# Node tables ahead of the sort's loop, and four PSUM banks for filter rows

## The chip, the cores and the metric

One core of a Trainium2 chip. The metric is the device time of one execution in microseconds; the kernel before took 6792.93 us (median of 3 runs, 6779.95 to 6798.9). The engines are TensorE (PE), VectorE (DVE), ScalarE (ACT), GpSimd (POOL) and SyncE (SP, which here only issues DMAs). Matrix inputs are float32 nearly everywhere.

## What is computed

A graph layer over 12,500 nodes of 256 features and 212,500 edges:

```python
h  = maximum(layernorm(x), 0)                      # LN without weights
xn = layernorm(h) * ln_w + ln_b
w  = (silu(rbf @ w1 + b1) @ w2 + b2) * cutoff[:, None]      # one row of 256 per edge
Q, K, V = xn @ wq + bq, xn @ wk + bk, xn @ wv + bv          # 8 heads of 32
attn = softmax over the 8 heads of (Q[src] . K[dst]) / sqrt(32) * cutoff
combined = xn[dst] * w + gate * attn * V[dst]
out = x + h + segment_sum(combined, src) @ wo + bo
```

## The kernel before

It has three stages: `prep`, `edges`, `finish`. The change is in `prep` alone.

`prep` sorts the edges by source node into 98 buckets of 128 nodes. Edges lie as 128 partitions x 1664 columns. In front of the loop, DVE counts 46 buckets (`tally`, L339) and ACT the others by sums of signs (L641). PE adds the counts over partitions and DVE makes the buckets' starts from them (L359 to L378). Then `first_chunk` ranks the edges of the first 128 columns: for each of the 98 buckets a comparison (`compare`, L385), a running count into PSUM (`count_up`, L393), a predicated copy of the rank into `pos` (L400) and a copy of the last count (L401). POOL clears the last unit of every bucket with 16 indirect DMAs (L284), and SP stores 25 MB of zeros behind the records (L232), ahead of its first four loads of edge attributes on the same queue.

The loop has 13 bodies of 16 groups; a group is 8 columns (1024 edges). Bodies are written once per entry of `SEGMENTS`, some as a hardware loop. Engines have their own instruction streams and meet at semaphores only. For each group:
- PE turns the attributes (`turn`, L540), computes the hidden layer of group g+1 in two halves (`hidden`, L551), and the filter rows of group g in four quarters j (`filters`, L562) into `w_ps[j % 2]`, two banks.
- ACT applies SiLU (L668), copies turned attributes (L659), and places cutoff, destination and slot beside the rows (L676, L677).
- DVE adds b2 and copies each quarter to `rows` (L505). Between quarters it ranks the next chunk of columns; chunks are (0,1), (1,3), (3,7), (7,11), (11,13) in bodies, so body 0 ranks 98 buckets over 256 columns, later bodies fewer.
- POOL scatters each of the 8 columns' rows to its slot in HBM by an indirect DMA (`scatter`, L303). `rows` is a ring of four groups.

The node tables ride in the same loop. A batch is 9 tiles of 128 nodes, 11 batches, one a body. In the body of a batch, ACT loads x; DVE takes statistics (L427, L434), POOL a power -1/2 (L292), DVE refines it (`normaliser`, L443 to L451), ACT makes h (L688), DVE and POOL do the same over h, DVE adds x + h (L469), ACT stores it as `base` and makes z (L700). In the next body DVE multiplies by ln_w (L478) and adds ln_b (L484), and at nine of the sixteen groups (`TILE_SLOTS`) PE turns one tile (L576) and multiplies it with wk, wv and wq (`node_tables`, L584 to L590), and ACT copies the results (L747, L708, L709, L711); then ACT stores the tables.

PSUM has eight banks: `rT_ps`, two of `hid_ps`, two of `w_ps`, `tq_ps`, `kv_ps`, `cs_ps`.

`edges` then reads the sorted records unit by unit with gathered table rows, and `finish` multiplies by wo.

Of the kernel before, what the change touches and what calls it, by code (L numbers as in the profile page):

```python
# [6 lines left out]
BF16 = mybir.dt.bfloat16  # L7
# [39 lines left out]
NB = 9  # L47
BATCHES = -(-BUCKETS // NB)
LASTB = BUCKETS - (BATCHES - 1) * NB
TILE_SLOTS = (3, 4, 6, 7, 9, 10, 12, 13, 14)  # L50
# [49 lines left out]
def prep(nc, sem, x, src, dst, rbf, weight, w1, b1, w2, b2, ln_w, ln_b, wq, bq, wk, bk, wv, bv, wo, bo,  # L100
         gate, recs, table, queries, base, ident, ones_bf, iota1, wos, bparts, unit_bucket, lagged_bucket, BQ, BKV):

    with ExitStack() as st:
# [3 lines left out]
        def ps(name, shape, dt=F32):  # L107
# [38 lines left out]

        xg = sb("xg", [P, NB, H])
        hg = sb("hg", [P, NB, H])
        stats = sb("stats", [P, NB, 6])
# [6 lines left out]
        kvx = sb("kvx", [P, NB, TAB])  # L156
        qf = sb("qf", [P, NB, H])
        xnT = sb("xnT", [P, 2, P])


        early = kvx[:].rearrange("p t f -> p (t f)")
        zero = early[:, 0:ZROWS * REC]
        unit_no = early[0:BUCKETS, ZROWS * REC:ZROWS * REC + UNITS]
        src_i = early[:, ZROWS * REC + UNITS:ZROWS * REC + UNITS + CPAD].bitcast(I32)
        dst_i = qf[:].rearrange("p t f -> p (t f)")[:, 0:CPAD].bitcast(I32)
        wgt = hg[:].rearrange("p t f -> p (t f)")[:, 0:CPAD]
        bucket_i = pos[:].bitcast(I32)
        tallied = hid[:].rearrange("p a b c e -> p (a b c e)")
# [10 lines left out]
        cs_ps = ps("cs_ps", [P, TMAX])  # L179

        s = {n: sem("a_" + n) for n in (
            "filled", "consts", "src_loaded", "edges_loaded", "params_loaded", "x_loaded",
# [4 lines left out]
            "stats_done", "stats_waited", "aggregated", "ve_done", "pow_done", "small", "h_done", "base_done", "base_stored", "z_done",  # L187
            "lnw_done", "xn_done", "xnt_ps", "xnt_sb", "kv_done", "kv_out", "q_done", "q_out", "table_stored", "q_stored")}
# [6 lines left out]
        SEGMENTS = ((0, 1), (1, 2), (2, 3), (3, 7), (7, 9), (9, 10), (10, 11), (11, 12), (12, 13))  # L195
# [10 lines left out]
        def tiles_of(batch):  # L206
            return LASTB if batch == BATCHES - 1 else NB
# [4 lines left out]
        def _(sp):  # L212
# [29 lines left out]
            for q in range(RING):  # L242
                load(q, q, None)
            with sp.Fori(1, GROUPS // RING - 1) as i:
                for q in range(RING):
                    load(i * RING + q, q, i * RING + q - RING + 1)
# [73 lines left out]
        def _(dve):  # L320
# [102 lines left out]
            def statistics(of, i, lo, h, a, b):  # L423
# [4 lines left out]
                if b < n:  # L428
                    return
# [773 lines left out]
```

## Time and profile before

| | us |
|---|---|
| median of 3 runs | 6792.93 |
| the profiled execution's own time | 6810.68 |
| its span, first to last instruction | 6809.0 |
| first row copy of the loop (L505) | 252.4 |
| end of the loop | 3152 |
| PE busy | 5942.5 (87%) |

The span is that of one profiled execution. A busy PE isn't PE at its peak, and the ends of its matmuls are modelled. "Idle before" is the time in which the engine did nothing just before an instruction; behind the arrow stands what released it. "issue" and "remote" name nothing that the profile knows by an instruction.

### The profile page before, as it was taken

The numbers are of one execution on the slowest core, as the hardware profiler recorded it, in microseconds if no ns is written. First come the engines' busy times: TensorE is split into PE (matmuls) and PEld (weight loads), VectorE is DVE, ScalarE is ACT, GpSimd is POOL, SyncE is SP. The second block draws the span as 40 slices with busy tenths as digits, with TensorE's granted clock in tenths as the row PEclk, the third lists the DMA queues.
The fourth block names the chain that finished last, engine by engine and source line by source line (L and its number), as shares of the span: only waits on it lengthen the run. The fifth ranks groups of instructions, "written<-read, shape, count | busy, mean of one in ns | idle before, by whom it ended". The sixth has DMA issues, their size and how long they took to land. (4 is left out here: it accounts for less than half of the span.)

```text
span 6809.0 us, 113345 instructions
## 1 busy us (share of the span) xinstructions
PE 5942.5 (87%) x25871; PEld 4370.4 (64%) x25872; DVE 4775.8 (70%) x12885; ACT 3086.9 (45%) x11532; POOL 3695.1 (54%) x3578
## 2 busy tenths in 40 slices
PE   0479988888898889885999999999999999999999
PEld 0356555555555555554777777777777777777776
DVE  8887755454534343222888889898888899888883
ACT  5123333333333333222655555565555565555552
POOL 1366665556555555554555555555555555555550
PEclk8799999999999999997999999999999999999999
DMA  8333333334333333335888888888888888888895
GB/s 296 102 107 112 128 136 132 108 117 138 134 109 121 137 134 103 125 127 185 287 284 284 283 281 285 286 287 283 286 283 283 283 285 286 285 284 285 284 271 158
DMA packets 487479, 1426.90 MB, mean 210 GB/s; under 512 B 76933, under 2 KB 154041, under 8 KB 484163
## 3 DMA queue, kind: packets, MB, share of 16 engines
q0 software_dynamic: 230240, 977.13, 43.7%
q1 hardware_dynamic: 206208, 370.53, 16.4%
q10 hardware_dynamic: 50850, 77.03, 3.2%
q8 instruction: 91, 1.49, 0.1%
q14 instruction: 90, 0.73, 0.0%
HBM read 1074.17 MB, written 350.21 MB: 209 GB/s over the span
## 5 line engine op out<-in xcount | busy, mean ns | idle before, releaser
L842 POOL DMA_INDIRECT ukvx<-kvx_table,udst x1856 | 1892.4, 1020 | 1588.4 <-DVE uav L1031 914.1
L303 POOL DMA_INDIRECT records<-rows,slot_i x1660 | 1727.1, 1040 | 1257.8 <-DVE rows L505 702.5
L562 PE MATMUL w_ps<-w2s,hid 128*128 128x256 f32 x6656 | 1631.7, 400 | 202.2 <-DVE rows L505 182.4
L562 PEld LDWEIGHTS w_ps<-w2s,hid 128*128 128x128 f32 x6656 | 1291.7, 200 | 566.9 <-DVE rows L505 228.5
L505 DVE TENSOR_TENSOR rows<-w_ps,b2b 128x512 f32<-128x512 f32 x832 | 569.7, 686 | 1384.4 <-PE w_ps L562 631.1
L668 ACT ACTIVATE hid<-hid_ps,b1t 128x512 f32<-128x512 f32 x832 | 525.6, 683 | 1483.8 <-PE hid_ps L551 719.4
L876 ACT ACTIVATE uexp<-uscores,umax 128x8 f32<-128x8 f32 x1856 | 542.4, 293 | 1377.6 <-issue 973.3
L930 PE MATMUL uq_ps<-aggr,uonehotT 128*128 (+1 forms) x3712 | 990.1, 389 | 137.3 <-issue 124.3
L939 PE MATMUL ag_ps<-uphys,uonehot_cut 128*128 128x256 f32 x3712 | 954.5, 380 | 0.1
L942 PE MATMUL ag_ps<-uav,uonehot 128*128 128x256 f32 x3712 | 953.6, 379 | 0.0
L989 DVE TENSOR_TENSOR uprod<-uq_ps,ukvx 128x512 f32<-128x512 f32 x928 | 640.3, 690 | 362.3 <-DMA ukvx<-kvx_table,udst 330.6
L930 PEld LDWEIGHTS uq_ps<-aggr,uonehotT 128*128 128x128 f32 x3712 | 634.1, 191 | 248.8 <-issue 194.6
L939 PEld LDWEIGHTS ag_ps<-uphys,uonehot_cut 128*128 128x128 f32 x3712 | 706.4, 190 | 96.8 <-issue 0.5
L942 PEld LDWEIGHTS ag_ps<-uav,uonehot 128*128 128x128 f32 x3712 | 706.3, 190 | 96.4
L947 PE MATMUL ag_ps<-aggr,ident 128*128 x1856 | 601.7, 406 | 124.1 <-ACT aggr L886 116.7
L551 PE MATMUL hid_ps<-rT,w1d 64*128 64x512 f32 x1664 | 485.4, 661 | 225.4 <-ACT hid L668 186.2
L1031 DVE TENSOR_TENSOR uav<-ukvx,attn_ps 128x512 f32<-128x512 f32 x928 | 637.5, 687 | 5.9
L867 ACT ACTIVATE uonehot_cut<-uonehot,urec 128x128 f32<-128x128 f32 x1856 | 635.2, 393 | 0.0
L994 DVE TENSOR_TENSOR uphys<-urec,ukvx 128x512 f32<-128x512 f32 x928 | 634.2, 683 | 0.1
L1001 DVE TENSOR_REDUCE uscores<-uprod 128x16 f32<-128x512 f32 x928 | 628.8, 678 | 0.0
L947 PEld LDWEIGHTS ag_ps<-aggr,ident 128*128 128x128 f32 x1856 | 298.4, 188 | 343.9 <-issue 313.0
L393 DVE TENSOR_TENSOR_SCAN cs_ps<-eq,run 128x512 f32<-128x512 bf16 (+2 forms) x494 | 453.2, 917 | 47.4 <-DVE run L401 23.2
(139 smaller groups left out, 6040.9 us busy)
## 6 DMA issues: line engine op xcount, KB each, us to landing
urec<-records SPq DMA_DIRECT2D x928, 260.0 KB
rbf_in<-in_edge_attr SPq DMA_DIRECT2D x207, 256.0 KB
kvx_table<-kvx ACTq DMA_DIRECT2D x10, 3456.0 KB
ukvx<-kvx_table,udst POOLq DMA_INDIRECT x1856
records<-rows,slot_i POOLq DMA_INDIRECT x1661
records<-kvx SPq DMA_DIRECT2D x1, 25480.0 KB
fbase<-x_plus_h SPq DMA_DIRECT2D x14, 896.0 KB, 7.2
out<-fout SPq DMA_DIRECT2D x13, 896.0 KB, 4.9
```

The lines of the kernel that those rows point to most:

```text
L303: pool.indirect_dma_start(recs, bass.IndirectOffsetOnAxis(ap=slot_i[:, q, t:t + 1], axis=0), rows[:, q, t, :], None).then_inc(scattered[q] ...
L562: m = pe.matmul(w_ps[j % 2][:, h, :], hid[:, k % 2, c, h, j * P:(j + 1) * P], w2s[:, c, :], start=(h == 0 and c == 0), stop=(c == 1), skip ...
L842: pool.indirect_dma_start(kvx[:, k % KVDEPTH, j, :], None, table, bass.IndirectOffsetOnAxis(ap=dst_i[:, k, j:j + 1], axis=0)).then_inc(kvx ...
L867: m = act.activation(ohc[:, k, j, :], oh[:, k, j, :], ACT.Copy, scale=rec[:, k, j, R_CUT:R_CUT + 1])
L930: m = pe.matmul(q_ps[k % 2][:, j, :], ohT[:, k % 2, j, :], aggr[:, bass.ds(b + QLAG, 1), :].rearrange("p a f -> p (a f)"), start=(j == 0), ...
L939: pe.matmul(ag_ps[k % 2][:, 0:H], ohc[:, k, j, :], phys[:, k % MDEPTH, j, :], start=(j == 0), stop=False)
L942: pe.matmul(ag_ps[k % 2][:, 0:H], oh[:, k, j, :], av[:, k % MDEPTH, j, :], start=False, stop=False)
L947: pe.matmul(ag_ps[k % 2][:, 0:H], ident[:], aggr[:, bass.ds(b, 1), :].rearrange("p a f -> p (a f)"), start=False, stop=True).then_inc(s["a ...
L989: dve.tensor_tensor(prod[:, q].rearrange("p (j h) d -> p j (h d)", j=2), q_ps[q][:], kvx[:, k % KVDEPTH, :, 0:H], ALU.mult).then_inc(s["qk ...
L994: dve.tensor_tensor(phys[:, k % MDEPTH], rec[:, k, :, 0:H], kvx[:, k % KVDEPTH, :, 2 * H:3 * H], ALU.mult).then_inc(s["phys_done"], 1)
L1001: dve.tensor_reduce(sc[:, q].rearrange("p j h -> p (j h)"), prod[:, q], AX_X, ALU.add).then_inc(s["scored"], 1)
L1031: dve.tensor_tensor(av[:, k % MDEPTH].rearrange("p j (h d) -> p j h d", h=NH), kvx[:, k % KVDEPTH, :, H:2 * H].rearrange("p j (h d) -> p j ...
```

## The change

The node tables are made in front of the loop, interleaved by hand with the tallies (batches 0 to 5), the starts (batch 6) and the first chunk's ranks (batches 7 to 13). There are 14 batches of 7 tiles; x, h and xn have two buffers each. On DVE: statistics, a third of the batch's tallies or ranks, the normaliser, a third, statistics of h, a third, and z (a two-scalar pass, ACT's before). On POOL: both powers, x + h, the products with ln_w and the sums with ln_b (DVE's before), and, in batches 8 to 11, four of the 16 indirect DMAs of zeros each. On ACT: Relu of batch b, and then the copies for the tiles of batch b-1, a share of the tallies ahead of each. On SP: all stores of base, xn, K/V and Q and the loads of x from batch 2 on. PE turns each tile one ahead and takes results into pairs of banks. The gate is multiplied into wv and bv once. The first ranks are made in fours, with four quarters of `cs_ps`. The loop keeps turn, hidden, filters, the row copies, the later chunks' ranks and the scatters, and `w_ps` has four banks, one for each quarter; `tq_ps` and `kv_ps` are gone. `SEGMENTS` has six entries, not nine.

```diff
-NB = 9
-TILE_SLOTS = (3, 4, 6, 7, 9, 10, 12, 13, 14)
+NB = 7
+THIRDS = ((0, 3), (3, 5), (5, 7))
...
-        w_ps = [ps(f"w_ps{k}", [P, 2, H]) for k in range(2)]
-        tq_ps = ps("tq_ps", [P, 4 * P])
-        kv_ps = ps("kv_ps", [P, 4 * P])
+        w_ps = [ps(f"w_ps{k}", [P, 2, H]) for k in range(4)]
+        xt_ps = [rT_ps, hid_ps[0]]
+        kv_ps = [hid_ps[1], w_ps[0][:].rearrange("p j f -> p (j f)")]
+        q_ps = [w_ps[k][:, 0, :] for k in (1, 2)]
...
-        SEGMENTS = ((0, 1), (1, 2), (2, 3), (3, 7), (7, 9), (9, 10), (10, 11), (11, 12), (12, 13))
+        SEGMENTS = ((0, 1), (1, 3), (3, 7), (7, 11), (11, 12), (12, 13))
...
# SP, behind the zeros and the first four loads of attributes
+            for b in range(BATCHES):
+                if b >= 1:
+                    sp.wait_ge(s["xn_done"], b)
+                    sp.dma_start(table[rows_of(b - 1), 2 * H:3 * H]..., xn[:, (b - 1) % 2])...
+                sp.wait_ge(s["base_done"], b + 1)
+                sp.dma_start(base[rows_of(b), :]..., xg[:, b % 2]).then_inc(s["base_stored"], 16)
+                if b >= 1:
+                    store_tables(b - 1)
+                if b + 2 < BATCHES:
+                    sp.wait_ge(s["base_stored"], b * 16 + 16)
+                    load_x(sp, b + 2)
...
# POOL
+            for b in range(BATCHES):
+                q = b % 2
+                power(b * 2 + 1, 0)
+                pool.wait_ge(s["h_done"], b * NB + NB)
+                pool.tensor_tensor(xg[:, q], xg[:, q], hg[:, q], ALU.add).then_inc(s["base_done"], 1)
+                power(b * 2 + 2, 1)
+                pool.wait_ge(s["z_done"], b * NB + NB)
+                pool.tensor_tensor(hg[:, q], hg[:, q], lnw_b..., ALU.mult).then_inc(s["lnw_done"], 1)
+                if b >= 2:
+                    pool.wait_ge(s["xnt_ps"], (b - 1) * NB)
+                    pool.wait_ge(xn_stored[q], b // 2 * 16)
+                pool.tensor_tensor(xn[:, q], hg[:, q], lnb_b..., ALU.add).then_inc(s["xn_done"], 1)
...
# DVE
+            for b in range(BATCHES):
+                a = [VBUCKETS * min(b * 3 + k, 18) // 18 for k in range(4)]
+                r = [28 * min(max((b - 7) * 3 + k, 0), 21) // 21 * 4 for k in range(4)]
+                first_statistics(b)
+                tallies(a[0], a[1])
+                ranks_first(r[0], min(r[1], BUCKETS))
+                normaliser(b, 0)
+                tallies(a[1], a[2])
+                ranks_first(r[1], min(r[2], BUCKETS))
+                if b == 0:
+                    split_biases()
+                if b == 6:
+                    starts()
+                second_statistics(b)
+                tallies(a[2], a[3])
+                ranks_first(r[2], min(r[3], BUCKETS))
+                standardise(b)
...
# PE
+            for b in range(BATCHES):
+                pe.wait_ge(s["xn_done"], b + 1)
+                node_turn(b, 0)
+                for t in range(NB):
+                    if t + 1 < NB:
+                        node_turn(b, t + 1)
+                    node_tables(b, t)
...
-                if not (isinstance(g, int) and g == 0 and j < 2):
-                    pe.wait_ge(s["w_out"], g * 4 + j - 1)
+                if not (isinstance(g, int) and g == 0):
+                    pe.wait_ge(s["w_out"], g * 4 + j - 3)
...
-                        m = pe.matmul(w_ps[j % 2][:, h, :], ...
+                        m = pe.matmul(w_ps[j][:, h, :], ...
...
# ACT
+            for b in range(BATCHES + 1):
+                share = [NT * min(b * NB + k, 6 * NB) // (6 * NB) for k in range(NB + 1)]
+                if b < BATCHES:
+                    rectify(b)
+                if b == 0:
+                    tallies(0, share[NB])
+                    act.wait_ge(s["meta_ready"], 4)
+                    continue
+                take_turned(b - 1, 0)
+                for t in range(NB):
+                    if t + 1 < NB:
+                        take_turned(b - 1, t + 1)
+                    tallies(share[t], share[t + 1])
+                    take_tables(b - 1, t)
```

`rectify(b)` waits for `small` of batch b and makes h; `take_turned` and `take_tables` wait for PE and copy; from batch 1 on `take_tables` also waits for the stores of the batch before. PE takes `totals`, `turn_ends` and `find_units` in batch 5, between tiles. DVE and ACT wait for `tails_zeroed` ahead of the loop.

## Rows read from the trace of the kernel before

**Rows 1.** Windows by stage: engines' busy us and count, clock, DMA share, GB/s.
```profile
0.00:109.00 109.00, 1.62 (x5) 1.10 (x6) 99.94 (x113) 89.65 (x108) 16.65 (x23) 1.00 0.82 300
109.00:252.40 143.40, 15.37 (x44) 6.49 (x44) 106.00 (x412) 6.37 (x11) 16.91 (x16) 0.58 0.61 186
252.40:3152.00 2899.60, 2555.95 (x10290) 1679.62 (x10288) 1432.29 (x2968) 900.56 (x2034) 1763.06 (x1677) 0.94 0.35 121
```

**Rows 2.** Timeline at the loop's start: start, us, engine, line, idle before.
```profile
250.45 2.08 PE L551 MATMUL hid_ps<-rT,w1d 64*128 64x512 f32 x4 [120.08 <-ACT hid L668]
```

**Rows 3.** Timeline of PE, 1063 to 1084: node tables, a clean group, a turn.
```profile
1063.20 0.38 PE L584 MATMUL kv_ps<-bparts,ones_bf 3*128 3x512 bf16 x1
...
1066.70 1.13 PE L551 MATMUL hid_ps<-rT,w1d 64*128 64x512 f32 x4
...
1076.52 1.13 PE L551 MATMUL hid_ps<-rT,w1d 64*128 64x512 f32 x4
...
1082.96 0.38 PE L576 MATMUL tq_ps<-ident,kvx 128*128 128x128 f32 x2
1083.18 3.62 PE L562 MATMUL w_ps<-w2s,hid 128*128 128x256 f32 x16
```

**Rows 4.** Groups by line, 0 to 3200: busy, mean ns, idle before, releasers.
```profile
L562 PE MATMUL w_ps<-w2s,hid 128*128 128x256 f32 x6656 | 1631.7, 400 | 202.2 <-DVE rows L505 182.4 <-issue 19.2
...
L688 ACT ACTIVATE hg<-xg,nb,rs 128x256 f32<-128x256 f32 x98 | 50.4, 589 | 19.8 <-DVE nb L451 19.8
...
L584 PE MATMUL kv_ps<-bparts,ones_bf 3*128 3x512 bf16 x98 | 40.1, 409 | 36.1 <-issue 19.7 <-ACT xnT L747 16.2
...
L427 DVE BATCH_NORM_STATS2 stats<-xg 128x6 f32<-128x256 f32 x98 | 34.0, 411 | 0.0
```

**Rows 5.** Timeline, 3004 to 3015, PE and ACT.
```profile
3004.44 1.13 PE L551 MATMUL hid_ps<-rT,w1d 64*128 64x512 f32 x4
...
3014.72 1.27 ACT L668 ACTIVATE hid<-hid_ps,b1t 128x512 f32<-128x512 f32 x2 [12.33 <-remote]
```

**Rows 6.** Groups of POOL: bodies 0 to 2; 3 to 10; 11 and 12.
```profile
L303 POOL DMA_INDIRECT records<-rows,slot_i x379 | 419.1, 1106 | 354.3 <-DVE rows L505 228.0 <-issue 116.2 <-ACT slot_i L677 10.1
...
L303 POOL DMA_INDIRECT records<-rows,slot_i x1023 | 1059.0, 1035 | 729.7 <-DVE rows L505 391.1 <-issue 300.4 <-ACT slot_i L677 38.2
...
L303 POOL DMA_INDIRECT records<-rows,slot_i x249 | 243.5, 978 | 173.2 <-DVE rows L505 87.3 <-issue 72.0 <-ACT slot_i L677 13.9
```

**Rows 7.** Timeline of DVE in body 0: scans with and without a row copy.
```profile
253.02 0.74 DVE L393 TENSOR_TENSOR_SCAN cs_ps<-eq,run 128x256 f32<-128x256 bf16 x1
...
254.85 0.76 DVE L393 TENSOR_TENSOR_SCAN cs_ps<-eq,run 128x256 f32<-128x256 bf16 x1
...
274.94 0.76 DVE L393 TENSOR_TENSOR_SCAN cs_ps<-eq,run 128x256 f32<-128x256 bf16 x1
...
276.45 0.76 DVE L393 TENSOR_TENSOR_SCAN cs_ps<-eq,run 128x256 f32<-128x256 bf16 x1
...
280.14 1.26 DVE L385 TENSOR_SCALAR eq<-bucket,ids 128x256 bf16<-128x256 bf16 x6
```

**Rows 8.** Front: tallies by line; POOL's copy; window of the first ranks.
```profile
L339 DVE TENSOR_SCALAR_CACHE_REDUCE eq<-bucket,ids 128x1664 bf16<-128x1664 bf16 x46 | 85.9, 1942 | 0.0
...
12.16 3.22 POOL L278 COPY meta<-hg 128x1664 f32<-128x1664 f32 x1 [0.96 <-DMA hg<-in_edge_weight]
...
150.00:200.00 50.00, 0.00 (x0) 0.00 (x0) 37.10 (x147) 0.00 (x0) 0.00 (x0) 0.50 0.92 265
```

**Rows 9.** SP's loads of attributes; the DMA packets of 16 to 60 us.
```profile
15.66 104.89 SPq L240 DMA_DIRECT2D rbf_in<-in_edge_attr  x6
...
DMA packets 1887, 14.50 MB, mean 329 GB/s; under 512 B 513, under 2 KB 1019, under 8 KB 1051
```

**Rows 10.** Windows of bodies 11 and 12.
```profile
2731.80:2950.80 219.00, 198.15 (x802) 131.02 (x801) 46.13 (x66) 62.24 (x142) 125.71 (x129) 0.94 0.35 121
2950.80:3144.30 193.50, 162.15 (x655) 110.04 (x653) 41.31 (x60) 47.83 (x105) 116.46 (x121) 0.90 0.32 110
```

More of the change, by code:

```diff
@@ L634, in _ @@
-            load_x(0, 0)
-            act.wait_ge(s["bucket_ready"], 3)
-            def tally(b, q, n):
-                if n is not None:
-                    act.wait_ge(s["counted"], n)
-                act.activation(tallied[:, q * CPAD:(q + 1) * CPAD], bucket[:], ACT.Sign, bias=cut[:, bass.ds(b, 1)],
-                               accum_out=above[:, bass.ds(b, 1)]).then_inc(s["counted"], 1)
-            for n in range(3):
-                tally(VBUCKETS + n, n % 2, n - 1 if n >= 2 else None)
@@ L645, in _, with tallies @@
-            with act.Fori(1, (BUCKETS - VBUCKETS) // 2) as i:
-                for q in range(2):
-                    tally(i * 2 + VBUCKETS + 1 + q, 1 - q, i * 2 + q)
+            load_x(act, 0)
+            act.wait_ge(s["src_loaded"], 32)
+            load_x(act, 1)
+            act.wait_ge(s["bucket_ready"], 3)
+            def tallies(begin, end):
+                for n in range(begin, end):
+                    b = VBUCKETS + n
+                    if n >= 2:
+                        act.wait_ge(s["counted"], n - 1)
+                    act.activation(tallied[:, (n % 2) * CPAD:(n % 2 + 1) * CPAD], bucket[:], ACT.Sign, bias=cut[:, b:b + 1],
+                                   accum_out=above[:, b:b + 1]).then_inc(s["counted"], 1)
@@ new lines, in rectify, with take_turned @@
+            def rectify(b):
+                act.wait_ge(s["small"], b * 10 + 5)
+                if b >= 2:
+                    act.wait_ge(s["xn_done"], b - 1)
+                for t in range(NB):
+                    act.activation(hg[:, b % 2, t, :], xg[:, b % 2, t, :], ACT.Relu, bias=nb[:, 0, t:t + 1], scale=rs[:, 0, t:t + 1]).then_inc(s["h_done"], 1)
+            def take_turned(b, t):
+                c = b * NB + t
+                act.wait_ge(s["xnt_ps"], c + 1)
+                if c >= 2:
+                    act.wait_ge(s["q_done"], c - 1)
+                act.activation(xnT[:, c % 2].rearrange("p k e -> p (k e)"), xt_ps[c % 2][:, 0:H], ACT.Copy).then_inc(s["xnt_sb"], 1)
@@ new lines, in take_tables @@
+            def take_tables(b, t):
+                c = b * NB + t
+                act.wait_ge(s["kv_done"], c + 1)
+                r = [lo for lo, _ in THIRDS].index(t) if b >= 1 and t in [lo for lo, _ in THIRDS] else None
+                if r is not None:
+                    act.wait_ge(kv_stored[r], b * 16)
+                act.activation(kv[:, t, :], kv_ps[c % 2][:, 0:2 * H], ACT.Copy).then_inc(s["kv_out"], 1)
+                act.wait_ge(s["q_done"], c + 1)
+                if r is not None:
+                    act.wait_ge(q_stored[r], b * 16)
+                act.activation(qf[:, t, :], q_ps[c % 2], ACT.Copy).then_inc(s["q_out"], 1)
```

461 lines of the change are left out of this document (220 added, 241 removed).

## The prediction

> **What bounds it now.** I read the windows by stage first [rows 1]. The span of 6809 us has three parts: a front (0 to 252), the sort's loop (252 to 3152, 2900 us), and the edge stage with the finish. The change doesn't touch the third. In the front TensorE (PE) does 17 us of work; it turns one group and then waits 120 us for the first chunk's ranks [rows 2]. In the loop PE is the busiest engine, 2556 of 2900 us. The timeline shows its cost where nothing waits [rows 3]: from one hidden matmul to the same one of the next group 9.82 us, and a node tile adds 0.22 us (two transposes) and 3.50 us (tables). So 208 x 9.82 = 2043 and 98 x 3.72 = 365 us are needed at full clock; the other 492 us of the loop are stalls: 344 us in which PE is idle (2900 less 2556), and about 148 us in which it is stretched (granted clock 0.94 on average). Of the idle time 202 us stand before filter matmuls, mostly released by DVE's row copies, 36 us before the node tables [rows 4]. The rest is uneven: now and then the engines behind PE start late though PE's records run on. ACT's activation at 3014.72 ends 12.33 us of idleness, while the hidden matmuls that it takes began at 3004.44 and lasted 1.13 us [rows 5]. I can't name the cause.
>
> **Moved away from the loop.** PE: 98 tiles, 365 us, and the 36 us of waits before them. ACT: Relu (50.4 us of records [rows 4]), z (as much), the copies of each tile, and the loads and stores of its queue. DVE: two rounds of statistics (34 us each), three wide passes and the normalisers. POOL: 22 powers of about 1.9 us. None of these engines is above 50% of the loop but POOL, and POOL loses least [rows 1]. If nothing else moved, the loop would be 2900 - 365 = **2535 us**.
>
> **Four banks of filter rows.** A filter matmul then waits for DVE's copy of the same quarter one group earlier, not two quarters earlier. That takes up delays of DVE of a few us. It gives nothing where PE itself is late or where hid_out is late. No row shows it; from below it gives 0, from above all 202 us. I take half, 101 us, since DVE loses its node passes too. With the 36 us this is 137 us of idle time; stretch follows idleness (148 / 344 = 0.43 us for each us), so another 59. That gives 2535 - 196 = 2339. I take **2360**, because of the next limits.
>
> **What is late next in the loop.** POOL issues eight scatters a group, 0.30 us apart. Their means are 1.106 us in bodies 0 to 2, 1.035 in 3 to 10, 0.978 in 11 and 12 [rows 6]: 11.25, 10.68 and 10.22 us a group, 48 x 11.25 + 128 x 10.68 + 32 x 10.22 = 2234 us. DVE in body 0 must rank 98 buckets: 1.84 us for one with a row copy between, 1.51 without, 0.21 for each compare (1.26 for six) [rows 7]. For 6.1 buckets a group this is 4 x 1.84 + 2.1 x 1.51 + 6.1 x 0.21 = 11.8 us, 189 us for the body against 227 now. So nothing below 2234 + 9 = 2243 is possible, and 2360 (11.3 us a group) is 5% above it.
>
> **The new front.** Per batch of seven tiles:
> - PE 7 x 3.72 = 26.0 us.
> - DVE: 14 statistics of 0.35 (34.0 / 98 [rows 4]), 14 aggregates of 0.08, two normalisers of 1.0, seven z passes, and small steps: about 10.5 us. z as a two-scalar pass of 256 columns has no row on DVE: I take 0.23 us, between nothing and the 0.41 of one statistics record. With 46 tallies (1.87 us apart) in six batches this is 24.8 us; with 98 ranks in seven batches, at 1.0 us each, it is 24.5 us; from 150 to 200 us DVE's 147 instructions (four a rank) are busy for 37.1 us, 1.01 a rank, and take 1.36 with their gaps, which ranks in fours should fill [rows 8].
> - ACT: Relu 3.6 (50.4 / 98 x 7 [rows 4]), copies 7 x 1.4 = 9.6, and nine tallies of 1.67 in the first six: 28 us, later 13.
> - POOL: two powers and three passes of 1792 elements. Its one-input copy of 1664 took 3.22 us [rows 8], so a pass costs from 3.5 us (a second input free) to 6.9 (twice). I take 4.5, nearer to the row; 17 us a batch.
>
> The longest is ACT's 28, then PE's 26. Each batch also has a turn: ACT rectifies batch b+1 ahead of the copies of batch b, and PE can run only two tiles ahead. I take **29.5 us a batch**. From below it is 26; from above the latency of one batch. From x to the last pass: 3.2 + 1.9 + 1.0 + 3.6 + 3.2 + 1.9 + 1.0 + 1.6 + 9 = 26 us, with 14 us of tallies between 40.
>
> The start: bucket numbers are ready at 12 us. Batch 0 then needs 26 us of latency, 13 us of tallies and 8 us of bias splitting, so its first tile is at about 58. Batch 2 comes much later. Its x is loaded by SP after base_stored of batch 0, and that store lies on SP's queue behind the 25480 KB of zeros and the first four rbf loads. Those loads are issued from 15.66 on, and from 16 to 60 us only 32 packets of 2 to 8 KB move (1051 - 1019), of 256 KB loads that have 128 each [rows 9]. The zeros move at 0.3 MB a us, so to about 105. So the store of base 0 lands at about 120, x of batch 2 at 128, its coefficients at 138. ACT rectifies batch 2 ahead of the copies of batch 1. So batch 1's tiles begin at about **141**, not at 87. The other 13 batches end at 141 + 13 x 29.5 = 525, and the loop's first row copy comes at 532: **+280 us** against 252.4. DVE's whole work from 128 on is some 300 us, so it isn't the bound. The stores (5 MB a batch) and the tail zeros (16 indirect DMAs, then in batches 8 to 11; now they hold the DMA at a share of 0.92 from 150 to 200 [rows 8]) share the DMA; they may add 10 to 20 us there, which the range takes in.
>
> **A rule that speaks against it.** POOL's copy beside DVE's first tally took 3.22 us and the tally 1.95, as the later ones (1.94) [rows 8]; but scatters are 13% longer where DVE has most work [rows 6]. The Trainium skill, "GPSIMD Engine Reference", section 8, says that GpSimd shares its SBUF interfaces with VectorE and meets contention with two-input or two-port instructions, and (section 3.1) gives 4497 ns for an add of 2048 elements. An estimate from that page is 3.9 us a pass, and twice this under contention. The trace has no two-input pass of that size on POOL. By the page's price the sum stays, since POOL is then at 15 us of 29.5; doubled it would be 27, and the front would go by the fourth case below.
>
> **The sum.** The profiled execution took 6810.7 us (span 6809.0 and 1.7 around it). 6811 + 280 - (2900 - 2360) = 6551. The median of the runs, 6792.9, is 18 us lower, so 6533.
>
> **Rivals.**
> 1. *Forecast*, 6533. For: 252 us of PE idleness in the front are filled. Chance 0.37.
> 2. *The stalls stay.* They belong to PE's own lateness [rows 5], not to banks; the loop takes 2535: 6811 + 280 - 365 - 18 = 6708. For: body 12 has no node work and still stalls [rows 10]. Chance 0.20.
> 3. *POOL becomes the bound.* Loop 2243: 6811 + 280 - 657 - 18 = 6416. For: the clean group of 9.82 lies under POOL's 10.2. Against: no body comes near it. 0.20.
> 4. *The front runs by latency*, 40 us a batch: 141 + 520 + 6 = 667, +415 us; 6811 + 415 - 540 - 18 = 6668. For: all four engines pass each batch on, twice through POOL. Its gain is gone only above 49.6 us a batch. 0.12.
> 5. *Slower: the bare network is itself slow.* Body 12 has neither node tiles nor ranks, and took 193.5 us for 15 groups, 12.9 each, more than body 11 with eight tiles less their 30 us (189 / 16 = 11.8) [rows 10]. If a loop without other work settles at that rate, it takes 189 + 192 x 12.9 = 2666: 6811 + 280 - 234 - 18 = 6839. It decides from (2620 - 189) / 192 = 12.66 us a group on. For: a clock of 0.90 and PE busy for 162 of 193 us. Against: part of that idleness is what four banks take up, and the loop as a whole less its tiles comes to 2535 / 208 = 12.2. 0.08.
> 6. *The zeros don't delay batch 2*, and batches take 27 us: 58 + 14 x 27 + 6 = 442, +190: 6443. 0.03.
>
> **The numbers.** Faster by over 0.3% (about what a measurement of this kernel can tell from no change, 20 us): cases 1 to 4 and 6, less a little for mixtures, 0.88; within it 0.03; slower 0.09. The range goes from 6400 (case 3 with 16 us off) to 6720 (case 2 with 12 more); case 5 is left out.
>
> **What would show it.** PE's first matmul of a tile near 58, a gap from about 87 to 141 with SP's load of batch 2 in it, 29.5 us from batch to batch, and the first row copy at 532. In the loop 11.3 us a group, filters hardly waiting on DVE, and POOL at 90% or more. A front beyond 600 us or groups of 12.7 us would make the forecast wrong; so would a late start that isn't SP's queue.

## The result: slower, and on the wrong side of the forecast

The changed kernel takes 6972.8 us (median of 4 runs) against 6788.5 of the kernel before beside it: a ratio of 1.0271, 95% interval 1.0245 to 1.0296. The forecast was 6533, with 6400 to 6720 as its range. The kernel before itself took 6779 to 6799 us (medians) in some of the comparisons and 6437 to 6446 in others, once the one and once the other on the same chip, and it kept to its level throughout a comparison but for one single run of 9832 us. I call the first **the stopping condition** and the second **the free condition**; each time below is compared with others of its own condition, unless the text says that it sets the two side by side. In the free condition the change is slower by 0.35% (1.0035, 1.0024 to 1.0047) and by 0.30% (1.0030, 1.0020 to 1.0041).

The first view of the changed kernel is the windows by stage (us, busy us and count of PE, PEld, DVE, ACT, POOL, then clock, DMA share and GB/s): the front to the first row copy (L568) at 612.9, the first body, the other twelve, and the whole loop.

```profile
138.00:612.90 474.90, 377.05 (x1121) 178.71 (x1121) 291.37 (x1005) 213.68 (x429) 189.78 (x74) 0.88 0.60 198
612.90:809.20 196.30, 164.18 (x712) 114.75 (x711) 174.54 (x453) 50.99 (x110) 130.92 (x125) 0.96 0.32 106
809.20:3327.90 2518.70, 2047.26 (x8412) 1405.42 (x8412) 1078.53 (x1958) 621.32 (x1337) 1535.37 (x1528) 0.89 0.30 100
612.90:3327.90 2715.00, 2211.43 (x9124) 1520.17 (x9123) 1253.07 (x2410) 672.31 (x1446) 1666.29 (x1652) 0.90 0.30 101
```

Against [rows 1] the front is 360.5 us longer (612.9 - 252.4; forecast 280) and the loop 184.6 us shorter (2899.6 - 2715.0; forecast 540). Together that is 176 us; the span grew by 162 (6970.8 - 6809.0), since what follows the loop was 14 us shorter. (Other runs with the same front had the first row copy at 598 to 620 us, so some ten of the 360 are scatter.) The loop runs at 13.05 us a group (2715 / 208) where I had 11.3.

Four banks did what they are for. The page's groups of the changed kernel:

```profile
L671 PE MATMUL w_ps<-w2s,hid 128*128 128x256 f32 x6656 | 1635.7, 401 | 38.0 <-issue 33.9
L774 ACT ACTIVATE hid<-hid_ps,b1t 128x512 f32<-128x512 f32 x832 | 527.1, 684 | 1992.2 <-remote 963.8
L660 PE MATMUL hid_ps<-rT,w1d 64*128 64x512 f32 x1664 | 527.8, 714 | 468.0 <-ACT rT L765 390.7
```

PE's idle time before the filters fell from 202.2 us [rows 4] to 38.0. It now stands before the hidden matmuls, 468.0 us, and ACT's SiLU waits 963.8 us for something remote. A stretch of the timeline in body 9 shows what it is (start, us, engine, line, idle before):

```profile
2525.32 3.72 PE L671 MATMUL w_ps<-w2s,hid 128*128 128x256 f32 x16
2525.62 0.69 DVE L568 TENSOR_TENSOR rows<-w_ps,b2b 128x512 f32<-128x512 f32 x1 [1.90 <-PE w_ps L671]
2529.16 1.13 PE L660 MATMUL hid_ps<-rT,w1d 64*128 64x512 f32 x4
2530.22 0.66 PE L649 MATMUL rT_ps<-ident,rbf_in 128*128 128x128 f32 x4
2534.87 0.69 DVE L568 TENSOR_TENSOR rows<-w_ps,b2b 128x512 f32<-128x512 f32 x1 [8.36 <-issue]
2535.57 0.38 PE L671 MATMUL w_ps<-w2s,hid 128*128 128x256 f32 x1 [0.95 <-issue]
2541.20 0.69 DVE L568 TENSOR_TENSOR rows<-w_ps,b2b 128x512 f32<-128x512 f32 x1 [4.97 <-remote]
2541.26 1.27 ACT L774 ACTIVATE hid<-hid_ps,b1t 128x512 f32<-128x512 f32 x2 [11.94 <-remote]
2541.47 0.33 SPq L254 DMA_DIRECT2D rbf_in<-in_edge_attr  x1
2543.15 1.22 PE L660 MATMUL hid_ps<-rT,w1d 64*128 64x512 f32 x2 [7.21 <-ACT rT L765]
```

The hidden matmuls are on record at 2529.16 and the turn at 2530.22. ACT, which waits for the first, and SP, which waits for the second, both start at 2541, within 0.3 us of each other and of DVE. Three engines that only share PE as their source are released together after 12 us. That is the puzzle of [rows 5] again: PE's matmuls are on record, but for a while the engines behind it get no sign of them (but for one row copy at 2534.87). PE's own records go on to 2535.95; then PE too does nothing until 2543.15, since it waits for ACT, which waits for PE. The trace doesn't tell whether the matmuls themselves were late or only the news of them. Windows of the same place show the clock:

```profile
2529.00:2537.50 8.50, 5.64 (x25) 3.64 (x24) 1.36 (x2) 0.33 (x3) 6.46 (x7) 1.00 0.30 109
2538.00:2548.00 10.00, 4.85 (x11) 2.82 (x12) 2.67 (x7) 3.23 (x7) 2.31 (x3) 0.50 0.18 60
```

First the halt begins under a granted clock of 1.00, with PE's records going on (5.64 us of 8.5), then comes a stretch at 0.50, which is 1.2 GHz. PE had been without work before the clock fell, so here the low clock comes behind the halt and doesn't start it. I call the pair **a stop**. In the changed loop about half of the groups take the clean 9.8 us; the stops lie in the others, of which many take 16 to 21 us.

### The profile page after: what moved, and what is told of

Its sections match the earlier page's. It is cut to its first block and busy times, and to the rows that moved or that the text cites. A ratio compares the mean times of both kernels' runs of the same rounds, so it can differ in the third digit from the quotient of the medians.

```text
span 6970.8 us, 114287 instructions
## 1 busy us (share of the span) xinstructions
PE 5982.0 (86%) x25871; PEld 4399.7 (63%) x25872; DVE 4768.5 (68%) x12989; ACT 3029.1 (43%) x11336; POOL 3799.3 (55%) x3626
## 5 line engine op out<-in xcount | busy, mean ns | idle before, releaser
L355 POOL DMA_INDIRECT records<-rows,slot_i x1660 | 1674.4, 1009 | 1102.1 <-issue 508.9
L568 DVE TENSOR_TENSOR rows<-w_ps,b2b 128x512 f32<-128x512 f32 x832 | 567.6, 687 | 1453.7 <-PE w_ps L671 736.3
L774 ACT ACTIVATE hid<-hid_ps,b1t 128x512 f32<-128x512 f32 x832 | 527.1, 684 | 1992.2 <-remote 963.8
L660 PE MATMUL hid_ps<-rT,w1d 64*128 64x512 f32 x1664 | 527.8, 714 | 468.0 <-ACT rT L765 390.7
L660 PEld LDWEIGHTS hid_ps<-rT,w1d 64*128 64x128 f32 x1664 | 137.7, 202 | 617.0 <-ACT hid L774 315.2
```

What stands on the lines that cost most here:

```text
L355: pool.indirect_dma_start(recs, bass.IndirectOffsetOnAxis(ap=slot_i[:, q, t:t + 1], axis=0), rows[:, q, t, :], None).then_inc(scattered[q] ...
L660: m = pe.matmul(hid_ps[h][:], w1d[half, c * P:(c + 1) * P], rT[half, k % 2, :], start=True, stop=True)
```

## Experiments

### What doesn't cause the stops

The stopping condition held (before: 6799). **A shorter code loop.** PE's loop is written over four groups a turn.

```diff
-            def body(i, lo):
-                for k in range(BODY):
+            def body(i, end):
+                for k in range(RING):
...
-            bodies(pe, body)
+            body(0, False)
+            with pe.Fori(1, GROUPS // RING - 1) as i:
+                body(i, False)
+            body(GROUPS // RING - 1, True)
```

> The changed kernel with TensorE's loop alone written over 4 groups a turn (50 turns) in place of 16, so that its code in the loop is a quarter; its work, order and waits are the same, and the other engines keep theirs. The loop of the changed kernel takes 13.05 us a group where PE's clean group is 9.8; in every third group the engines behind PE start 8 to 13 us late. Theory S (PE's instructions run out: 90 KB of loop code can't be supplied at the 9.0 instructions a us of a clean group, and a quarter of it can): the late starts go, 10.8 to 11.3 us a group, 6520 to 6620 us. Theory P (the late starts come when PE has worked without a pause for some 25 us, whatever its code): nothing changes, 6973 within 25 us, as many late starts.

Measured: 6989.8 us, 1.0279 (1.0255 to 1.0304), the loop 2704.6 us. That is theory P's forecast. Theory S falls: the size of PE's loop code isn't the cause.

**Two banks again.**

```diff
-                if not (isinstance(g, int) and g == 0):
-                    pe.wait_ge(s["w_out"], g * 4 + j - 3)
+                if not (isinstance(g, int) and g == 0 and j < 2):
+                    pe.wait_ge(s["w_out"], g * 4 + j - 1)
...
-                        m = pe.matmul(w_ps[j][:, h, :], ...
+                        m = pe.matmul(w_ps[j % 2][:, h, :], ...
```

> The changed kernel with two banks for filter rows in place of four (as in the kernel before), nothing else. Theory P: a filter matmul waits for the row copy two before it, PE pauses more often and the late starts get fewer; the two about cancel, 12.7 to 13.3 us a group, 6900 to 7025 us. Theory F (four banks do what they are for and the late starts have nothing to do with PE's pauses): the 202 us of waits for filter banks that the kernel before had come back on top of the 13.05, 7120 to 7180 us.

Measured: 7037.8 us, 1.0346 (1.0312 to 1.0381), some 50 us over x1 in the same comparison, between the two forecasts. Four banks are worth a few tens of us in this condition, not the 144 that they were priced at (101 of waits and 0.43 of that in stretch).

**A wait for each quarter.**

```diff
-                if not (isinstance(g, int) and g == 0):
-                    pe.wait_ge(s["w_out"], g * 4 + j - 3)
+                if not (isinstance(g, int) and g == 0 and j == 0):
+                    pe.wait_ge(s["w_out"], g * 4 + j)
```

> The changed kernel with four banks still, but each filter quarter of PE waits for the row copy of the quarter just before it, so that PE pauses some 0.9 us twice to four times a group. Theory P: PE is paced to about 11.8 us a group, as in body 0 of the changed kernel where VectorE paced it to 11.7 with hardly a late start; the late starts go, 11.6 to 12.3 us a group, 6670 to 6820 us. Theory S gives the same (7.5 instructions a us). Theory F: the pauses come on top, 2 to 3 us a group more, 7380 to 7600 us.

Measured: 7147.7 us, 1.0516 (1.0490 to 1.0542). Outside both ranges. The windows of bodies 1 to 6, and of 7 to 12:

```profile
901.60:2127.50 1225.90, 1010.79 (x4224) 657.29 (x4224) 705.46 (x1176) 311.10 (x675) 806.50 (x771) 0.98 0.32 105
2127.50:3479.90 1352.40, 1041.25 (x4196) 669.90 (x4196) 393.83 (x782) 305.35 (x662) 731.03 (x761) 0.96 0.27 93
```

In bodies 1 to 6 the clock is 0.98 and the median group takes 11.9 us, in all 12.8 a group (1225.9 / 96), under the changed kernel's 13.2 (1264.7 / 96). In bodies 7 to 12 it is 14.1, and body 0 took 17.6, since there PE waits behind DVE's ranks. So there is less time at 1.2 GHz with these pauses (0.98 and 0.96 against 0.89 and 0.90 in the changed kernel), but the loop as a whole is longer. This kernel has no run in the free condition, so how much of its loop is pause and how much is stops stays open.

**More dense work.** The hidden matmuls of the first half are done twice.

```diff
-                for h in range(2):
+                for h in (0, 1) if c else (0, 1, 0, 1):
```

> The changed kernel with the pair of hidden matmuls of the first half (64 rows by 512 columns each) done twice with the same result: 8 more PE instructions of over 0.6 us a group and no pause more. PE's clean group grows from 9.8 to some 11.2 us, at 8.6 instructions a us instead of 9.0. Theory S: fewer instructions a us, the late starts thin out, 11.6 to 12.8 us a group, 6680 to 6920 us. Theory P: PE still never pauses, the late starts stay as frequent in time, 14.2 to 15 us a group, 7210 to 7380 us.

Measured: 7012.1 us, 1.0291 (1.0250 to 1.0332). The clean group is 10.67 us, 0.85 more than 9.82, but the loop grew by 43 us (2757.5 - 2714.3, first to last row copy) where 0.85 x 207 is 176. Against x1, which ran beside it, the loop grew by 53 us and the median by 22. Both theories priced this wrongly: dense work added within the loop cost a third of its clean time at most. Why is not shown; a fixed rate of 13 us a group would be one reading, and the pause further down speaks against it.

### The same kernels in the free condition

The next comparison met the free condition (before: 6446). **One pause a group, two pauses, thin work.**

```diff
                     if more2:
                         turn(g + 2, k + 2, i, end and k + 2 == BODY - 1)
+                    if more2:
+                        pe.wait_ge(s["rT_out"], g + 3)
                     filters(g, k, 2)
```

> The changed kernel, and PE waits once a group, ahead of its third filter quarter, for ScalarE's copy of the features that it has just turned (two groups ahead of their use). ScalarE has the SiLU of the hidden half (1.26 us) and that copy (0.6) to do in that time, so PE pauses some 1.4 us in each group and its clean group becomes 11.2 us. Theory A (an unbroken run of dense matmuls brings a stop of completions and then a stretch at 1.2 GHz; a pause each group keeps both away): 11.2 to 11.9 us a group, 6590 to 6740 us. Theory C (PE's real throughput on this work is about 13 us a group, whatever the records of the clean groups say, and the late starts are its backlog): the pause is hidden in the backlog, 13.0 to 13.3 us a group, 6960 to 7030 us. Theory F (late starts independent of what PE does): 14.4 us a group, 7260 us.

x6 has a second wait ahead of the first filter quarter, `pe.wait_ge(s["hid_out"], g * 2 + 3)`.

> As the last one, and a second pause a group: PE waits ahead of the first filter quarter for the SiLU of the next group's first hidden half (some 1.4 us after its matmul). Clean group 12.6 us. Theory A: no late starts at all, 12.6 to 12.8 us a group, 6880 to 6930 us, slower than one pause. Theory C: 13.0 to 13.4 us a group, 6960 to 7050 us. Theory F: 15.8, 7540 us.

x7 has no wait, but work of three rows:

```diff
+                for _ in range(4 if j == 2 else 0):
+                    pe.matmul(w_ps[2]..., ones_bf[0:3, :], bparts[:, BKV], start=True, stop=True, ...)
```

> The changed kernel, and in place of a pause PE does four more matmuls in each group ahead of its third filter quarter, of 3 rows by 512 columns in bf16 (0.41 us each in the front), whose result is overwritten. PE's group becomes about 11.45 us with no pause in it, but the added columns go through 3 rows of the array in place of 128. If the late starts hang on how many rows and passes the array really works on (dense work), they go as in x5: 11.4 to 12 us a group, 6640 to 6760 us. If they hang on the share of time in which PE is busy, they stay as frequent: 13.2 to 15 us a group, 7000 to 7380 us.

Measured: 6631.2 us (11.4 us a group), 6989.4 (13.1) and 6551.0 (11.0), nearly all groups alike, and hardly a stop to be kept away. They can't judge theory A. So the changed kernel was run again, beside two of them.

> The changed kernel itself again, beside the kernel before on this chip. Two chips have shown two times for the kernel before: 6799 us on the first, 6446 on the second, where the loop of the variant with the zeros spread took 10.5 us a group and hardly a stretch at 1.2 GHz. Theory A (what a chip takes of dense matmuls without a stop differs from chip to chip): where before takes 6799, this takes 6950 to 7000 with 13 us a group; where before takes 6446, this takes 6455 to 6475 with 10.5 us a group and a first row copy at 600 to 613 us. Rival (the change is 2.7% slower on any chip): 6620 where before takes 6446.

Measured: 6456.9 us against 6437.4, 1.0035 (1.0024 to 1.0047), within the forecast, on the chip of the first experiments, where the kernel before had taken 6799. What stops PE is then no fixed property of a chip; it comes and goes.

> The kernel with one pause of PE a group for ScalarE's copy of the features, as before, to have it beside the changed kernel on one chip. Theory A: if before takes about 6799 here, the pause keeps the stops away: 11.4 to 12 us a group, 6640 to 6760 us, 200 to 330 us less than the changed kernel; if before takes about 6446, 6631 within 15, 160 to 180 us more than the changed kernel. Theory C (the array's real throughput is 13 us a group where before takes 6799): 6960 to 7030 us there.

Measured: 6630.4 us. Without stops the pause is a plain loss of 174 us. (Bodies 1 to 12 took 2184.2 us in place of 1989.0, 195 more; what follows the loop was 20 us shorter.)

> The kernel with four thin matmuls (3 rows by 512 columns, bf16) added to each group, beside the changed kernel on one chip. If before takes about 6799 here and the stops hang on the rows that really work: 11.0 to 11.7 us a group, 6560 to 6700 us; if they hang on PE's busy time alone: 13 to 14 us a group, 6960 to 7200 us. If before takes about 6446: 6551 within 15.

Measured: 6553.2 us, 96 us over the changed kernel.

**Both kernels' traces side by side.**

> The kernel before itself, for its trace beside the changed kernel's. Where it takes about 6440 us: the front ends at 252 us as it did, and the loop takes 2530 to 2560 us in place of 2900; Theory A (what went are the stops that unbroken matmuls bring): the waits for filter banks (202 us) stay about as they are, what is missing are the 148 us of clock stretch and the late starts behind PE. Rival: the filter-bank waits go as well, since the slower engines behind PE caused them. Where it takes about 6800 us: as the first trace, within 20 us.

> The changed kernel, beside the others of this call. Theory A: 6973 within 30 where the kernel before takes about 6800; 6457 within 12 where it takes about 6440.

Measured: 6444.0 (ratio to the other runs of before 1.0000) and 6462.3, 1.0030 (1.0020 to 1.0041). The forecast for the loop of the kernel before (2530 to 2560) came in, and with it the rival: PE's waits for filter banks went as well. They are, in the stopping and then in the free condition (total, times, longest):

```profile
PE w_ps L562 <- DVE rows L505: 182.4, 76, 9.9
```

```profile
PE w_ps L562 <- DVE rows L505: 67.2, 20, 10.4
```

So of the waits that four banks were to take up, 115 us were there only because of the stops. Windows of the loop: the kernel before, then the changed kernel (body 0, the rest, the whole; from c_after), both in the free condition. Few stretches at 1.2 GHz are left in these loops, but not none:

```profile
248.60:2781.00 2532.40, 2441.38 (x10290) 1629.10 (x10288) 1438.23 (x2968) 898.20 (x2034) 1772.98 (x1670) 0.98 0.41 138
```

```profile
601.20:794.40 193.20, 164.66 (x712) 115.38 (x711) 174.23 (x454) 51.00 (x110) 130.82 (x125) 0.97 0.32 108
794.40:2783.40 1989.00, 1903.70 (x8412) 1333.66 (x8412) 1041.44 (x1958) 617.96 (x1337) 1523.69 (x1512) 0.99 0.38 126
601.20:2783.40 2182.20, 2068.37 (x9124) 1449.04 (x9123) 1215.67 (x2410) 668.96 (x1446) 1654.52 (x1636) 0.99 0.37 124
```

This is the core of the case. Each kernel's loop in both conditions:

| loop, us | stopping | free | stops cost |
|---|---|---|---|
| kernel before | 2899.6 | 2532.4 | 367 |
| changed kernel | 2715.0 | 2182.2 | 533 |

The counts are equal (10290 and 9124 matmuls), so only time differs. In the free condition the change takes 350 us out of the loop and puts 353 into the front (601.2 - 248.6): nothing is won. In the stopping condition the loop without node tiles pays 166 us more for stops than the one with them, and that is nearly all of the 2.7% (184 us). Why it pays more is not shown. PE's busy share doesn't explain it: in the free condition it is 96% in the loop of the kernel before (2441 of 2532 us) and 95% in the changed one (2068 of 2182). Nor do all stages with a busy PE have stops: behind the loop PE is busy for 3370 us of 3657 at a clock of 0.99 in the stopping condition, and of 3670 in the free one.

How the 533 us divide is an estimate. PE's busy time grew by 143 us (2211.4 - 2068.4) and its idle time by 390. The clock can have cost some 245 us at most (0.90 in place of 0.99: 0.09 x 2 x 2715 = 490 us more at 1.2 GHz, half of it lost if PE had work all that time). At least half of the price is PE standing idle. The kernel before had a rhythm of 9.8, 13.5, 13.5 us in the free condition, 9.82 and 9.82 + 3.72, the prices of [rows 3].

In the later part of the changed kernel's loop (80 groups, from 1815 to 2629 us, in the free condition) the loop has found its next bound:

```profile
ACT rows L782 <- DMA records<-rows,slot_i: 439.8, 79, 6.1
DVE rows L568 <- DMA records<-rows,slot_i: 372.0, 62, 7.7
```

```profile
L355 POOL DMA_INDIRECT records<-rows,slot_i x640 | 619.7, 968 | 194.9 <-issue 185.2 <-DVE rows L568 9.7
```

ACT and DVE wait for scatters to land, and POOL's issues are 0.968 us with 0.30 between: 8 x 1.27 = 10.2 us a group, as measured (814 / 80). That was the third case. Body 0 took 193.2 us, against 189 in my estimate of DVE.

### The pause where there are stops

The last comparison met the stopping condition again, on a third chip (before: 6779.0). f6_front and f6_pause differ in the wait of x5 alone.

> As f6_front, with one pause of PE a group (the wait of c_x5). Theory A where the kernel before takes about 6800: 11.4 to 12 us a group beside 13 of f6_front, 6550 to 6680 us; Theory C there: 13 us a group, the same as f6_front within 40. Where the kernel before takes about 6440: 11.4 us a group beside 10.5, 6535 to 6560 us.

Measured: 7120.1 us, 1.0500 (1.0474 to 1.0525), against 6923.4 for f6_front. Windows of the loop, first f6_front, then f6_pause in the stopping condition, then the same loop in the free one (f5_front_pause):

```profile
565.00:3281.70 2716.70, 2202.92 (x9124) 1515.12 (x9122) 1252.55 (x2410) 672.26 (x1446) 1662.97 (x1651) 0.90 0.30 101
```

```profile
564.90:3474.80 2909.90, 2206.94 (x9124) 1522.68 (x9123) 1266.41 (x2410) 669.78 (x1446) 1672.12 (x1650) 0.91 0.28 94
```

```profile
551.20:2929.00 2377.80, 2091.91 (x9124) 1440.90 (x9123) 1255.72 (x2409) 667.94 (x1446) 1676.65 (x1651) 1.00 0.34 115
```

The stops cost 2909.9 - 2377.8 = 532 us with the pause, as many as the 533 without it, though PE's busy share in the free condition is only 88% with the pause (2092 of 2378 us). Both forecasts of f6_pause missed. Theory A falls in the form that I gave it: a pause of some 1.5 us in each group takes nothing off their total. Theory C falls with it, since the pause isn't hidden either; the loop pays its whole 193 us.

### The front

**Zeros spread.** (Free condition.)

```diff
-                if BATCHES - 6 <= b < BATCHES - 2:
-                    for c in range((b - BATCHES + 6) * ZPIECES // 4, (b - BATCHES + 7) * ZPIECES // 4):
+                if b >= BATCHES - 7:
+                    for c in range((b - BATCHES + 7) * ZPIECES // 7, (b - BATCHES + 8) * ZPIECES // 7):
```

> The changed kernel with GpSimd's 16 scatters of zeros to the records (some 26 MB) issued over batches 7 to 13 of the front (two or three each) in place of four each in batches 8 to 11. In the changed kernel the DMA engines are 0.90 busy from 400 to 500 us and batch 11 takes 66 us where the others take 32. Theory D (the base row and table stores and the load of x queue behind those 26 MB): batch 11 falls to 35 to 45 us, the first row copy comes 20 to 40 us sooner, 6930 to 6955 us. Rival (batch 11 waits for something else, its own ring of buffers): within 8 us of 6973. The loop is untouched.

Measured: 6427.3 us, 0.9981 (0.9970 to 0.9992), the first row copy at 567.2 against 601 in c_after: 34 us, as theory D had it. The changed kernel (its first trace) from 400 to 500 us, and f1 there:

```profile
400.00:500.00 100.00, 60.44 (x170) 28.03 (x168) 42.87 (x191) 24.42 (x57) 37.06 (x18) 0.81 0.90 278
```

```profile
400.00:500.00 100.00, 85.69 (x252) 40.52 (x252) 82.38 (x321) 39.26 (x90) 51.98 (x22) 0.91 0.88 290
```

At nearly the same DMA share PE does 252 matmuls in place of 170. (The changed kernel in the free condition, c_after, does 183 there at a DMA share of 0.95.) The waits of the changed kernel's front (total, times, longest) name what had queued behind the zeros, one load of x (40.4 us) and one store of tables (22.5; in c_after the longest such waits are 9.0 and 14.3); the other two rows are PE's, for the first tile and in batch 1:

```profile
DVE stats L401 <- DMA xg<-in_x: 99.5, 4, 40.4
ACT kv L733 <- DMA kvx_table<-kv: 22.5, 1, 22.5
PE rT_ps L605 <- POOL xn L336: 68.2, 2, 64.1
PE w_ps L613 <- ACT xnT L725: 72.9, 7, 34.0
```

**ReLU later.** ScalarE's `rectify(b)` is moved behind the first tile's tables of batch b-1, on top of f1.

> The changed kernel with two edits of the front: the scatters of zeros spread over batches 7 to 13, and ScalarE's seven ReLU passes of batch b issued after the first tile's tables of batch b-1 in place of ahead of them, where ScalarE waited some 10 us a batch for VectorE's numbers while PE waited for ScalarE. Theory: the batch is then bound by PE's 23 to 26 us of tiles or VectorE's 25, so 13 batches of 26 to 29 us, and the first row copy comes at 485 to 530 us in place of 565 to 613; 6860 to 6900 where the changed kernel takes 6973, 6340 to 6390 where before takes 6446. Rival (batches are bound by the chain of one batch through VectorE, GpSimd and back): 32 us a batch stay, only the zeros' 35 us are gained.

Measured: 6410.7 us, 0.9960 (0.9946 to 0.9974), the first row copy at 557.0. Ten us more, not the 37 to 82 of the theory: the rival, 34 us a batch.

**VectorE's order.** f4 has `standardise(b)` directly behind `second_statistics(b)`; f5 is f4 with the pause; f6 puts the third share of ranks with the second.

> The changed kernel with the two edits of f3_front and a third: VectorE standardises batch b (seven passes that GpSimd's second half waits for) directly after its second statistics, and ranks four buckets after that in place of ahead of it. In f3_front the batches from the seventh on took 34 us, which is the way of one batch from its ReLU by VectorE's statistics, 7.6 us of ranks, the standardising and GpSimd's two passes to PE's first tile and on to the next batch's ReLU. Theory: that way gets 7.6 us shorter, 26 to 28 us a batch, the first row copy at 490 to 515 us in place of 557; 6350 to 6375 where the kernel before takes 6440, 6840 to 6880 where it takes 6800. Rival (VectorE is full by then): 32 to 34 us a batch stay, the first row copy at 540 to 560.

> The kernel f4_front and one pause of PE a group (the wait of c_x5). Its front is that of f4_front, so that the loop is read apart. Where the kernel before takes about 6800, Theory A: the pause keeps the stops away, 11.4 to 12 us a group in place of 13, 6530 to 6660 us, faster than the kernel before; Theory C (the array's real throughput is about 13 us a group there): 13 us a group, 6840 to 6880 us. Where it takes about 6440: 11.4 us a group in place of 10.5, 6520 to 6550 us.

> The changed kernel with the zeros spread, the ReLU after the first tile (both as f3_front) and, in VectorE's order of a batch, the third share of tallies and ranks put with the second, ahead of the second statistics; the standardising then follows them with nothing between. In f4_front a share of ranks stood behind the standardising, where four comparisons that take 0.25 us each lasted 8.3 us, to the end of GpSimd's two passes; here the statistics of the next batch stand there, which kept their 0.41 us beside such passes. Theory: 28 to 30 us a batch from batch 7, first row copy at 505 to 530 us in place of 557; 6365 to 6385 where the kernel before takes 6440, 6860 to 6900 where it takes 6800. Rival (the sum of VectorE's work and its waits for GpSimd's power is the bound, in whatever order): 33 to 35 us a batch, 6400 to 6415. Loop as in the changed kernel: 10.5 us a group where before takes 6440, 13 where it takes 6800.

Measured: 6412.3 us for f4 (0.9946, 0.9929 to 0.9962; first row copy 551.6), 6584.1 for f5 (its loop at the pause's 11.4 us a group, as forecast, and its front at f4's 551, yet 34 us above the range of 6520 to 6550, which was added up from the front that f4 was to have), and for f6, in the stopping condition, 6923.4 (1.0208, 1.0184 to 1.0232; 565.0). Three orders of the same work gave 34 to 37 us a batch in most of the later batches, where the theories of f4 and f6 had 26 to 30. The rival is right for f3 and f4, and nearest for f6 (33 to 35 forecast, 35 to 38 measured): DVE was busy for 172.35 of 200 us (f6, 300 to 500), and waits for POOL's powers come on top. Part of that busy time is no work. The timeline of the changed kernel, DVE and POOL:

```profile
291.83 1.03 DVE L407 TENSOR_SCALAR ve<-mv 128x7 f32<-128x7 f32 x1
292.77 4.43 DVE L486 TENSOR_SCALAR eq<-bucket,ids 128x128 bf16<-128x128 bf16 x4
293.00 3.99 POOL L336 TENSOR_TENSOR xn<-hg,lnb_b 128x1792 f32<-128x1792 f32 x1 [0.17 <-POOL hg L331]
```

Four compares that take 0.74 us elsewhere last 4.43 here, until POOL's pass ends at 296.99; in f4, where they met both passes, 8.34 us (397.26 to 405.60, POOL from 397.43 to 405.55). The Trainium skill, "SBUF — State Buffer", section "SBUF: two separate sides", says that a GpSimd instruction and a VectorE instruction in a 2-port mode or with two SBUF inputs hold the shared ports exclusively, for the whole instruction, and that the one that comes second blocks. The traces agree for these compares as far as they go: they end with POOL's pass. The statistics of 256 columns kept their 0.41 us beside the same passes. Which mode an instruction ran in, no trace here shows.

In the free condition f1, f3 and f4 are 0.2 to 0.5% faster than the kernel before. In the stopping one they were not run; f6_front, the nearest to them, was 2.1% slower there, and none of the kernels that were run in it beat the kernel before.

## Why the prediction was wrong, step by step

- **The clean prices** (9.82 a group, 3.72 a tile) were right, as the free condition's rhythm of 9.8 and 13.5 us shows.
- **The failed step is the treatment of the 492 us of stalls.** I took them as idle time that a looser wait takes up, and let the clock's stretch shrink with it (0.43 us for each us). 367 us of them were stops, which more banks and fewer interruptions don't remove. They cost 533 in the changed loop. Even the waits for filter banks, of which I took half, were mostly their doing: 67.2 us stand there without stops, 182.4 with them. The step "2535 - 196 = 2339" went the wrong way: 2182 + 533 = 2715. Without stops the forecast would have failed as well: the loop of the kernel before then holds 2532 - 2408 = 124 us of stalls, not 492, and the change gives 350 us, not 540.
- **Case 2** named the kind (PE's own lateness) but held the stalls constant. **Case 5** had the mechanism, the bare network slow by itself at body 12's rate of 12.9; it decides from 12.66 us a group on behind body 0, and 13.1 was measured there (2518.7 / 192). It was the rightest case and had 0.08. But the rate belongs to the stopping condition: in the free one the same groups take 10.4 us (1989.0 / 192). Its evidence [rows 10] and the timeline of [rows 5] lay open; my counterargument, that the loop less its tiles comes to 12.2, took for granted that the tiles' time is simply subtracted.
- **Case 3**, POOL as the bound, is what the free condition shows for a good third of the loop: 10.2 us a group. I had 10.68 for bodies 3 to 10 from scatters of 1.035 us; they were 0.968 there.
- **The front** came to 612.9, not 532. The first tile waited for xn until 64.1 us (forecast 58). PE waited 34.0 us in batch 1 and was in its tiles from 134 on (forecast 141; the queue of SP was right, the load of batch 2 was issued at 115.65). The other batches took 35.8 us each ((600 - 134) / 13) where I had 29.5, and from the last table to the first row copy it was 13 us, not 7: -7 + 13 x 6.3 + 6 = 81, the 81 us missed. Of them 34 are the zeros by f1 (I had "10 to 20"). The division of the rest is an estimate: about 10 for the totals and unit tables (42.7 us from the first tile of batch 5 to that of batch 6, where its neighbours took 32), and for the others batches of some 32.5 us, with DVE blocked by POOL's passes in part of them. Those passes were 3.98 us, where I took 4.5 and the page's price gave 3.9; the doubling under contention was my own assumption, and no run shows it. I had looked for contention in the passes and not in VectorE, which pays it.
- **Case 4**, latency, was half right: 35.8 lies between 29.5 and 40.

**What stays open.** I didn't find what sets the condition, nor what starts a stop. The size of PE's loop code, two banks in place of four (the clock was 0.91 over that loop) and PE's busy share don't explain them; one pause a group changes nothing in total, though x3's bodies 1 to 6 were at 12.8 us a group and its bodies 7 to 12 at 14.1, with the same work on PE. Body 0, which DVE paces to 11.7 us, loses only 3 us to the stops (196.3 against 193.2). The Trainium skill, "TensorE: Matmul & The Clock Gate", section "Seeing it yourself", describes a limiter that brings a whole die to 13/16 of the clock when three of its cores do dense matmuls. The clock records of these traces show 0.5 and 1.0 only, and the kernel keeps one core busy, so it is not that in the form described; whether neighbours on the chip play a part couldn't be tried with a kernel on one core. The thin work of x7 was never tried in the stopping condition.

## What to carry to other kernels

Before you price a stall at what a looser wait would give, look at whether the engines behind PE are released together and late; such time isn't waiting that a looser condition takes up, and it can make waits elsewhere look longer than they are. Moving PE work out of a PE-bound loop wins only what the new place hides: here 350 us went out and 353 came in, since the front's batches ran at some 35 us for 26 us of PE work. Measure the kernel before beside each experiment, since a chip's level can move by 5% from one comparison to the next.

## What the runs showed of the hardware

- One program has two levels, 6437 to 6446 and 6779 to 6799 us, on the same chip at different times; the difference lies in the sort's loop (367 us); what follows the loop took 3657 us in the one and 3670 in the other.
- In the stop shown, ACT, DVE and SP get hardly a sign of PE's matmuls for 12 us. PE's records go on for the first 7 of them at a granted clock of 1.00, then PE stands idle, and a stretch at 0.50 follows.
- What the stops cost didn't follow PE's busy share: 367 us at 96%, 533 at 95%, 532 at 88% (share in the free condition). Behind the loop PE is busy for 92% and there are none to be seen.
- Dense work added to such a loop cost a quarter to a third of its clean time (43 or 53 of 176 us), a pause its whole (193 us, and 195 without stops).
- Four bf16 compares of 128 columns on VectorE lasted until the end of GpSimd's pass with two inputs beside them: 4.43 and, across two passes, 8.34 us in place of 0.74.
- GpSimd issued the indirect scatters at 0.968 us with 0.30 between: with eight of them a stage is bound at 10.2 us a group.
